# Ternary weights cast and summed in front of self attention, fp8 weights early, and a GpSimd wait at the attention seam

## The chip, the core and the metric

The kernel runs on one core of a Trainium2 chip. The metric is device time in microseconds for one execution, the median of several runs. TensorE (PE) does matrix products into PSUM, VectorE (DVE), ScalarE (ACT) and GpSimd (POOL) do elementwise work and reductions, SyncE (SP) issues most DMA transfers. Each engine runs its own list of instructions in order; semaphores hold an instruction until others are done.

## The reference

Eight residual stages run over x of 16 x 64 tokens and 256 features, each on the layer norm of x; `ctx` has the same shape.

```python
x = x + _L0_xattn_ref(16, 64, 256, L0_xattn_w, L0_xattn_u, _layernorm(x, axis=-1), ctx_2048)   # a decayed scan
x = x + _L0_ffn_ref(_layernorm(x, axis=-1), L0_ffn_W_gate, L0_ffn_W_qkv)                       # self attention, gated keys
x = x + _L1_xattn_ref(_layernorm(x, axis=-1), ctx_2048, ...)                                   # cross attention, int8 rounding
x = x + _L1_ffn_ref(_layernorm(x, axis=-1), L1_ffn_input2, L1_ffn_scale, L1_ffn_scale1)        # fp8 product
x = x + _L2_xattn_ref(_layernorm(x, axis=-1), ctx_2048, ctx_2048)                              # channel attention
x = x + _L2_ffn_ref(_layernorm(x, axis=-1), L2_ffn_w_gate_up, L2_ffn_w_proj)                   # ternary weights
x = x + _L3_xattn_ref(...)
x = x + _L3_ffn_ref(...)                                                                       # eight experts
```

The ternary weights of the sixth stage depend on no activation:

```python
w = w_fp32.astype(jnp.bfloat16)
w_g = w.reshape(-1, g)                                        # groups of 64
scale = jnp.clip(jnp.mean(jnp.abs(w_g), axis=-1, keepdims=True), 1e-08, None)
q = jnp.clip(jnp.round(w_g / scale), -1, 1)
w_hat = (q * scale).reshape(w.shape)
return w + jax.lax.stop_gradient(w_hat - w)
```

## The kernel before

The 1024 tokens are eight tiles of 128 (NT is 8). X holds the residual, XN the norms, both in SBUF throughout; `region` and `wide` are two large SBUF buffers out of which every stage cuts its own tiles. Each engine has one function per stage, called in order of the stages, so that the order of work on an engine is written out by hand, and semaphores tie the engines together. `x_done` counts finished residual tiles over all stages: the first stage ends at `x_done` 8. `ch.link` makes an instruction wait for the one before it on its own engine.

Self attention and cross attention are `pe_attention`, `act_attention`, `vec_attention` and `pool_attention` with s = 0 and s = 1. Each runs over the tiles with a fixed lag per step: `key_value` (TensorE), `select` (VectorE, from L703), key copy (`key_T`, L619, ScalarE), key blocks (`kbd`, L422, GpSimd), `scores` (L525, TensorE), `shift` (L737 and L740, VectorE), `probs` (L625), `probs_T`, `values` (L553), `normalise` (from L752). At the seam between the two, VectorE normalises and quantises the new tokens in halves: `quantise_norm` (L355 to L700), where TensorE waits for the second half in `quantised_T(1, 4)` ahead of the third scores. In the slot before that seam VectorE rounds the fp8 weights (`vec_f8_weights`, L838 to L396). GpSimd also splits the context into bf16 parts, a step per tile (`pool_context_part`, L991 to L999), adds biases to the values (L445) and fills a block with constants (`pool_blank_keys`).

Channel attention goes over 64 pairs of units in `pair_steps`: at pair w VectorE takes the maxima of its scores (L1171, two per pair); TensorE makes the scores of pair w (L1057) and, 13 pairs behind, the turned scores (L1081) and the values (L1097); ScalarE makes the exponentials (L1111). Three score banks are shared, so TensorE stops when VectorE has taken no maxima. Every eight pairs the maxima go through DMAs into the stack (`maxima_in`). Results go out to DRAM and come back per tile (`act_values_out`, `values_in`); VectorE inverts the sums (`invert`, L1187) and GpSimd multiplies and adds to X (`add_values`, L1153 and L1155).

The ternary weights are six chunks of 128 x 1024. Each is loaded (L1221 and L1225, ScalarE's queue, into two buffers in `wide`), cast to bf16 on ScalarE (L1231), summed by groups (L1241), scaled (L1243 to L1245), compared above and below (L1249, L1251) on VectorE, and put together by GpSimd (L1258 to L1261). Chunks 0 and 1 stand in front of VectorE's pair loop, 2 and 3 inside it, 4 and 5 after the second inversion. In `pe_ternary` TensorE turns the finished weights when all six are there; the stage's norm waits for all of X.

## Time and profile before

| what | us |
|---|---|
| median of 3 runs | 876.08 (875.85 to 881.13) |
| profiled execution | 883.72 |
| its span, first to last instruction | 881.9 |
| busy: PE / DVE / ACT / POOL | 653.6 / 519.7 / 285.3 / 248.6 |
| mean granted TensorE clock | 0.853 of full |

Times in the trace count from the start of the span of that one execution. The timeline lists instructions in order of time, several of one line in a row merged; a table of stretches gives busy time per engine between two times; groups by line add up instructions of one source line.

### The profile page before, as it was taken

What the parts mean: (1) busy time and instruction counts of PE and PEld (TensorE: products, weight loads), DVE (VectorE), ACT (ScalarE), POOL (GpSimd) and SP (SyncE); (2) the same over time, 40 slices, a digit from 0 to 9 for tenths busy, and PEclk for the clock granted to TensorE, in tenths of its full rate; (3) what the DMA queues carried; (4) which work ended last, traced back from release to release, by engine and by line L of the source; (5) the groups of instructions that cost most, each with busy time, mean ns of one, the idle gap of its engine ahead of it and who ended that gap; (6) DMA issues with size and microseconds to landing.
All of it is one profiled execution on the core that took longest, in us unless ns stands there. A gap on an engine that the chain in (4) does not pass through costs nothing.

```text
span 881.9 us, 10923 instructions
## 1 busy us (share of the span) xinstructions
PE 653.6 (74%) x3659; PEld 415.5 (47%) x3660; DVE 519.7 (59%) x1102; ACT 285.3 (32%) x522; POOL 248.6 (28%) x244
## 2 busy tenths in 40 slices
PE   2634888756883168989639996754599999999991
PEld 2323344533562115555334665524266666666661
DVE  6986687797969899998955444564321221212213
ACT  4811322313447106666624321331121121211210
POOL 3220432275901396130670005000212111121100
PEclk9665998677986559999958999975699999999996
DMA  7000003000206624561210002966000000000004
GB/s 239 0 0 1 0 1 72 1 1 0 61 1 156 157 70 107 136 169 47 66 48 1 1 1 99 430 267 253 24 19 30 30 24 24 25 30 30 18 12 156
DMA packets 34142, 61.85 MB, mean 70 GB/s; under 512 B 6232, under 2 KB 29784, under 8 KB 31768
## 3 DMA queue, kind: packets, MB, share of 16 engines
q1 hardware_dynamic: 22592, 45.78, 16.5%
q10 hardware_dynamic: 9296, 9.44, 3.5%
q0 software_dynamic: 2208, 6.03, 2.2%
q8 instruction: 26, 0.43, 0.2%
q14 instruction: 20, 0.16, 0.1%
HBM read 47.35 MB, written 13.50 MB: 69 GB/s over the span
## 4 chain that ended last, share of the span: by engine, by line
PE 48%; DVE 22%; issue 7%; POOL 5%; ACT 3%; DMA 1%; ACTq 0%; POOLq 0%; SPq 0%; DVEq 0%
PE bank L1746 16%; PE bank L1767 8%; PE bank L1386 5%; DVE region L1171 4%; PE bank L1405 3%; DVE XN L355 2%; PE bank L1757 2%; PE bank L553 2%; PE bank L525 2%; PE bank L1097 2%; PE bank L1057 1%; ACT region L1445 1%; PE bank L537 1%; POOL rstd L369 1%; PE bank L1081 1%
## 5 line engine op out<-in xcount | busy, mean ns | idle before, releaser
L1746 PE MATMUL bank<-region,wide 128*128 x368 | 144.0, 545 | 0.3 <-issue 0.3
L1650 DVE TENSOR_TENSOR wide<-wide,bank 128x448 f32<-128x448 f32 x46 | 28.6, 621 | 125.3 <-ACT wide L1693 125.3
L1746 PEld LDWEIGHTS bank<-region,wide 128*128 128x128 f32 x368 | 68.9, 192 | 61.6 <-issue 61.5
L1111 ACT ACTIVATE region<-bank 128x1024 f32<-128x1024 f32 x64 | 65.6, 1026 | 67.7 <-PE bank L1081 64.7
L1171 DVE TENSOR_REDUCE region<-bank 128x2 f32<-128x512 f32 x128 | 79.8, 678 | 7.1 <-PE bank L1057 6.9
L1767 PE MATMUL bank<-region,XN 128*128 x322 | 73.4, 379 | 1.2 <-DVE wide L1663 1.2
L1554 POOL DMA_INDIRECT choice_results<-wide,to_row x23 | 22.7, 987 | 181.6 <-DVE wide L1663 181.6
L1057 PE MATMUL bank<-region 128*128 128x256 bf16 x256 | 52.8, 305 | 20.4 <-DVE region L1171 15.9
L1767 PEld LDWEIGHTS bank<-region,XN 128*128 128x128 f32 x322 | 59.5, 190 | 9.3 <-issue 2.1
L1693 ACT ACTIVATE wide<-bank 128x448 f32<-128x448 f32 x46 | 25.0, 543 | 112.2 <-PE bank L1746 112.2
L369 POOL TENSOR_TENSOR rstd<-vareps,half_neg 128x4 f32<-128x4 f32 (+1 forms) x13 | 16.2, 1246 | 145.8 <-DVE vareps L365 96.3
L1881 PE MATMUL bank<-ident,XN 128*128 128x128 f32 x96 | 20.8, 398 | 42.0 <-DVE XN L355 26.5
L1657 DVE COPY XN<-bank 128x384 f32<-128x384 f32 x23 | 12.8, 557 | 63.2 <-PE bank L1757 63.2
L1386 PE MATMUL bank<-region 128*128 128x512 bf16 x192 | 44.3, 389 | 0.9 <-DVE region L404 0.9
L1097 PE MATMUL bank<-region 128*32 128x256 f32 x512 | 34.3, 383 | 12.9 <-ACT wide L1120 12.5
L1057 PEld LDWEIGHTS bank<-region 128*128 128x128 bf16 x256 | 19.8, 101 | 49.0 <-DVE region L1171 34.7
L553 PE MATMUL bank<-wide,region 128*64 128x34 f32 x512 | 33.4, 239 | 11.6 <-issue 8.8
L553 PEld LDWEIGHTS bank<-wide,region 128*64 128x64 f32 x512 | 32.0, 154 | 18.7 <-issue 15.8
L1881 PEld LDWEIGHTS bank<-ident,XN 128*128 128x128 f32 x96 | 17.9, 211 | 44.5 <-issue 26.9
L1081 PE MATMUL bank<-region 128*128 128x256 bf16 x256 | 38.2, 275 | 0.0
L1700 ACT ACTIVATE XN<-bank 128x512 f32<-128x512 f32 x23 | 13.7, 597 | 73.0 <-PE bank L1757 73.0
L422 POOL TENSOR_TENSOR region<-wide 128x1024 f32<-128x1024 f32 x16 | 30.5, 1925 | 22.0 <-DVE XN L700 11.4
(305 smaller groups left out, 1279.8 us busy)
## 6 DMA issues: line engine op xcount, KB each, us to landing
region<-in_L_ffn_experts_dram SPq DMA_DIRECT2D x8, 2688.0 KB, 19.2
region<-ctx_parts SPq DMA_DIRECT2D x24, 192.0 KB
region<-norm_parts SPq DMA_DIRECT2D x24, 192.0 KB
channel_values<-wide ACTq DMA_DIRECT2D x8, 512.0 KB, 4.4
ctx_parts<-region SPq DMA_DIRECT2D x40, 64.0 KB, 2.1
wide<-in_L_ffn_w_gate_up_dram ACTq DMA_DIRECT2D x4, 512.0 KB, 7.1
wide<-channel_values SPq DMA_DIRECT2D x16, 128.0 KB, 2.6
norm_parts<-region SPq DMA_DIRECT2D x24, 64.0 KB, 4.6
```

Of the source, the lines that this page charges most:

```text
L422: last = e.tensor_tensor(KBD[i % 2][c], src.unsqueeze(1).broadcast_to([P, HC, P]), headmask.unsqueeze(2).broadcast_to([P, HC, P]), ALU.mult)
L553: last = e.matmul(ps(4 + i % 2, w * j, w * j + w)[T * b:T * b + T, :], PT[:, P * j + T * b:P * j + T * b + T], VBD[i % 2][:, b, 0 if s == ...
L1057: last = e.matmul(score_bank("scores", n)[:, D * mc:D * mc + D], QS[i % RING][:, n % TU, P * mc:P * mc + P], KS[i % RING][:, n % TU, :], s ...
L1081: last = e.matmul(ps(2 + 2 * (w % 2) + u, D * nc_, D * nc_ + D), KS[i % RING][:, n, P * nc_:P * nc_ + P], QS[i % RING][:, n, :], start=Tru ...
L1097: last = e.matmul(ps(6, 0, D)[32 * g:32 * g + 32, :], flat[:, 2 * DH * n:2 * DH * n + 32], PT5[(2 * q + g // 2) % 4][:, 512 * (g % 2) + D ...
L1111: e.activation(PT5[w % 4], bank[1 + w % 2][:, :], ACT.Exp, scale=QSCALE).then_inc(s_chan["probs_ready"], 1)
L1171: e.tensor_reduce(nmax[i % 2][:, at_:at_ + KC], score_bank("scores", n).rearrange("p (c n) -> p c n", c=KC), AX.X, ALU.max, negate=True).t ...
L1386: last = e.matmul(bank[hf][:, 512 * gu:512 * gu + 512], x6[j][:, c, P * i:P * i + P], guT[:, c, lo:lo + 512], start=(j == 0 and c == 0), s ...
L1650: e.tensor_tensor(HB8[par][:, cols], silu8[:, cols], bank[hf][:, 512:512 + I8 // 2], ALU.mult)\
L1746: last = e.matmul(bank[hf][:, 512 * gu:512 * gu + hw], xbT[par][:, P * c:P * c + P], region[:, bass.ds(off + (2 * gu + c) * I8 + hw * hf, ...
L1767: last = e.matmul(ps(7, 0, D), HT8[par][:, P * k:P * k + P], region[:, bass.ds(off + 4 * I8 + D * k, D)], start=(k == 0), stop=(k == I8 // ...
L1881: last = e.transpose(ps(first + c, P * j, P * j + P), src[:, D * i + P * c:D * i + P * c + P], ident[:, :])
```

## The change

The six chunks get six buffers of their own, in the place of the later key stacks 2 and 3 and the fill block in `region`. SP loads them all behind the fp8 weights, when the first residual is done, and issues the context parts after that. ScalarE casts the chunks ahead of the loop of self attention, around its first gate sum and its query copies. VectorE rounds the fp8 weights and makes the sums of chunks 0 and 1 before the first `select`, the sums of the other four and the scales of all after it. In channel attention only the two comparisons of each chunk are left on VectorE, at pairs 3 and 4, 12 and 13, and so on every nine; nothing of the ternary weights is in front of the loop or behind it. GpSimd puts all six chunks together before it adds any values, and VectorE adds the last tile's values itself. At the seam GpSimd waits for all quantised norms before it goes on with the context parts and key block 2.

```diff
-        traw = [wide[:, TCH * j:TCH * j + TCH] for j in range(2)]
+        traw = [carve(TCH, at=STACK * 2 + TCH * c) for c in range(TW // TCH)]
...
                     if i == 1:
                         pool_norm(e, 2, 4, NT)
+                        e.wait_ge(s_att["norm_quantised"], NT)
                     pool_context_part(e, ch, 1, i - 1)
...
             if s == 0:
-                gate_sum(0)
-                leave(QT, 0, s_att["q_in_psum"], s_att["q_ready"])
+                for c in range(TW // TCH):
+                    if c == 2:
+                        gate_sum(0)
+                    if c == 4:
+                        leave_half(QT, 0, 0, s_att["q_in_psum"], s_att["q_ready"])
+                    act_ternary_cast(e, c)
+                leave_half(QT, 1, KC, s_att["q_in_psum"], s_att["q_ready"])
...
+                if s == 0 and t == 0:
+                    vec_f8_weights(e, ch)
+                    for c in range(2):
+                        vec_ternary_sums(e, ch, c)
                 if s == 0 and t < NT:
                     select(t)
+                if s == 0 and t == 0:
+                    for c in range(2, TW // TCH):
+                        vec_ternary_sums(e, ch, c)
...
                 if s == 0 and t == NT + 1:
                     quantise_norm(0, 4)
-                if s == 0 and t == NT + 2:
-                    vec_f8_weights(e, ch)
                 if s == 0 and t == NT + 3:
                     e.wait_ge(x_done, 2 * NT)
                     norm_variance(e, ch, 2, 4, NT, first=NT - 1)
...
             act_blanks(e, KS[2:4], True)
-            for c in range(2):
-                act_ternary_load(e, c)
             e.wait_ge(s_att["projected"], NT)
             act_blanks(e, QS[0:2], False)
             turned_f8(0)
             act_blanks(e, QS[2:4], True)
-            for c in range(2):
-                act_ternary_cast(e, c)
-                act_ternary_load(e, c + 2)
...
         def values_in(e, i):
             e.wait_ge(s_chan[f"values_stored{i % 2}"], 16 * (i // 2 + 1))
-            if i == 2:
-                e.wait_ge(s_tern["weights_cast"], 5)
             if i >= SETS:
                 e.wait_ge(x_done, 4 * NT + i - SETS + 1)
             v = o_dram[i].rearrange("q (g r) d -> (q g) r d", g=4)
...
             if i == RING:
+                e.wait_ge(s_tern["weights_cast"], TW // TCH)
                 ch.link(e.memset(fill5[0:32, :].bitcast(U32), 0))
             elif i == RING + 1:
...
-            def weights(w):
-                if w in CASTS:
-                    c = CASTS[w]
-                    act_ternary_cast(e, c)
-                    if c + 2 < TW // TCH:
-                        act_ternary_load(e, c + 2)
-
-            CASTS = {8: 2, 16: 3, 24: 4, 32: 5}
-            pair_steps([(weights, 0), (probs, BEHIND), (values, BEHIND + 2), (values_out, BEHIND + 2)])
+            pair_steps([(probs, BEHIND), (values, BEHIND + 2), (values_out, BEHIND + 2)])
...
         def pool_channel_tiles(e, ch):
-            WEIGHTS = {0: (0, 1, 2, 3), 2: (4,), 4: (5,)}
             for i in range(2, NT):
                 e.wait_ge(s_chan["norm_split"], i)
                 split_q(e, ch, i, qrest[1])
-            for i in range(NT):
-                for c in WEIGHTS.get(i, ()):
-                    pool_ternary_weights(e, ch, c)
+            for c in range(TW // TCH):
+                pool_ternary_weights(e, ch, c)
+            for i in range(NT - 1):
                 add_values(e, ch, i)
 
         def add_values(e, ch, i):
             e.wait_ge(s_chan["sums_inverted"], i + 1)
             ch.link(e.tensor_tensor(NUM5[i % SETS], NUM5[i % SETS], DEN5[i % SETS], ALU.mult))
+            if i == NT - 1:
+                e.wait_ge(x_done, 4 * NT + i)
             xi = X[:, D * i:D * i + D]
             e.tensor_tensor(xi, xi, NUM5[i % SETS], ALU.add).then_inc(x_done, 1)
 
         def vec_channel(e, ch):
-            WEIGHTS = {17: 2, 35: 3}
-            for c in range(2):
-                for step in range(4):
-                    vec_ternary_step(e, ch, c, step)
+            SIGNS = {9 * c + 3: c for c in range(TW // TCH)}
...
             def weights(w):
-                for first, c in WEIGHTS.items():
-                    if 0 <= w - first < 4:
-                        vec_ternary_step(e, ch, c, w - first)
+                for step in range(2):
+                    if w - step in SIGNS:
+                        vec_ternary_signs(e, ch, SIGNS[w - step], step)
 
             pair_steps([(maxima, 0), (maxima_parts, 1), (weights, 0)])
             for i in range(NT):
                 invert(i)
-                if i == 1:
-                    for c in (4, 5):
-                        for step in range(4):
-                            vec_ternary_step(e, ch, c, step)
+            add_values(e, ch, NT - 1)
...
-        def act_ternary_load(e, c):
-
-            if c >= 2:
-                e.wait_ge(s_tern["weights_cast"], c - 1)
+        def sp_ternary_load(e, c):
...
+                e.dma_start(traw[c].rearrange("p (r d) -> p r d", d=D),
                             L2_ffn_w_gate_up[P * rows * c:P * rows * (c + 1), :].rearrange("(r p) d -> p r d", p=P))\
-                    .then_inc(s_tern[f"weights_loaded{c % 2}"], 16)
...
         def act_ternary_cast(e, c):
-            e.wait_ge(s_tern[f"weights_loaded{c % 2}"], 16 * (c // 2 + 1))
-            if c == 0:
-                e.wait_ge(x_done, 3 * NT)
-            e.activation(tern[:, ternary_slices(c)[0]], traw[c % 2], ACT.Copy).then_inc(s_tern["weights_cast"], 1)
-
-        def vec_ternary_step(e, ch, c, step):
+            e.wait_ge(s_tern[f"weights_loaded{c // 2}"], 32)
+            e.activation(tern[:, ternary_slices(c)[0]], traw[c], ACT.Copy).then_inc(s_tern["weights_cast"], 1)
+
+        def vec_ternary_sums(e, ch, c):
+            cols, g = ternary_slices(c)
+            e.wait_ge(s_tern["weights_cast"], c + 1)
+            last = e.tensor_reduce(tscale[:, g], by_group(tern[:, cols]), AX.X, ALU.add, apply_absolute_value=True)
+            if c == TW // TCH - 1:
+                ch.link(last)
+                ch.link(e.tensor_scalar(tscb, tscale, 1.0 / GROUP, 1e-8, ALU.mult, ALU.max))
+                e.tensor_scalar(thigh, tscb, 0.5 + 2.0 ** -9, None, ALU.mult)
+                ch.link(e.tensor_scalar(tlow, tscb, -(0.5 + 2.0 ** -9), None, ALU.mult))
+
+        def vec_ternary_signs(e, ch, c, step):
 
             cols, g = ternary_slices(c)
             w = tern[:, cols]
             if step == 0:
-                e.wait_ge(s_tern["weights_cast"], c + 1)
-                if c == 0:
-                    e.wait_ge(x_done, 4 * NT)
-                ch.link(e.tensor_reduce(tscale[:, g], by_group(w), AX.X, ALU.add, apply_absolute_value=True))
-            elif step == 1:
-                ch.link(e.tensor_scalar(tscb[:, g], tscale[:, g], 1.0 / GROUP, 1e-8, ALU.mult, ALU.max))
-                e.tensor_scalar(thigh[:, g], tscb[:, g], 0.5 + 2.0 ** -9, None, ALU.mult)
-                ch.link(e.tensor_scalar(tlow[:, g], tscb[:, g], -(0.5 + 2.0 ** -9), None, ALU.mult))
-            elif step == 2:
                 if c >= 2:
                     e.wait_ge(s_tern["weights_ternary"], c - 1)
                 e.tensor_tensor(by_group(tpos[c % 2]), by_group(w), spread(thigh[:, g]), ALU.is_gt)
...
-            for i in range(NT // 2):
-                sp_context_parts(e, i)
             e.wait_ge(x_done, NT)
...
-            for i in range(NT // 2, NT):
+            for c in range(TW // TCH):
+                sp_ternary_load(e, c)
+            for i in range(NT):
                 sp_context_parts(e, i)
             sp_first_keys(e)
```

## Rows read from the trace of the kernel before

**Rows 1.** Timeline, front of self attention: start us, us, engine, line, operation, out<-in, count
```profile
74.92 1.28 DVE L2037 TENSOR_TENSOR X<-X,bank 128x512 f32<-128x512 f32 x2
...
79.52 1.38 DVE L355 TENSOR_SCALAR XN<-X,meanvar,rstd 128x256 f32<-128x256 f32 x4 [1.19 <-POOL rstd L369]
...
87.05 0.17 DVE L711 COPY region<-bank 128x16 f32<-128x16 f32 x1 [6.15 <-PE bank L491]
...
94.41 0.27 ACT L619 ACTIVATE region<-bank 128x128 f32<-128x128 f32 x1
```
**Rows 2.** Stretches: us, busy PE PEld DVE ACT POOL (instructions), PEclk, DMA share, GB/s
```profile
2.50:20.00 17.50, 3.70 (x17) 3.43 (x17) 13.18 (x41) 8.93 (x14) 5.20 (x13) 0.96 0.89 300
...
176.70:185.70 9.00, 7.93 (x40) 5.01 (x40) 8.72 (x11) 1.37 (x2) 6.46 (x5) 0.69 0.01 2
...
304.50:314.30 9.80, 0.00 (x0) 0.00 (x0) 9.59 (x14) 0.00 (x0) 9.08 (x11) 0.50 0.60 134
...
333.00:418.00 85.00, 75.40 (x797) 46.60 (x798) 77.15 (x142) 57.59 (x77) 23.44 (x12) 1.00 0.46 116
```
**Rows 3.** Timeline, the seam between self and cross attention
```profile
167.34 1.37 DVE L355 TENSOR_SCALAR XN<-X,meanvar,rstd 128x256 f32<-128x256 f32 x4
...
172.31 1.14 DVE L700 TENSOR_SCALAR XN<-XN,region 128x256 f32<-128x256 f32 x4
...
185.80 3.65 PE L525 MATMUL bank<-region 128*64 128x512 f32 x16 [0.98 <-ACT region L1966]
...
188.04 1.22 DVE L737 TENSOR_REDUCE region<-bank 128x16 f32<-128x1024 f32 x1
...
189.28 1.04 POOL L991 CAST region<-region 128x1024 bf16<-128x1024 f32 x1
...
190.40 3.80 POOL L422 TENSOR_TENSOR region<-wide 128x1024 f32<-128x1024 f32 x2
190.43 6.84 DVE L355 TENSOR_SCALAR XN<-X,meanvar,rstd 128x256 f32<-128x256 f32 x4
...
203.95 1.14 DVE L700 TENSOR_SCALAR XN<-XN,region 128x256 f32<-128x256 f32 x4
...
207.11 3.15 PE L525 MATMUL bank<-region 128*64 128x512 f32 x8
...
241.78 2.88 PE L525 MATMUL bank<-region 128*64 128x512 f32 x8
```
**Rows 4.** Groups by line, VectorE, 333 to 418: count, busy us, mean ns, idle before, releaser
```profile
L1171 DVE TENSOR_REDUCE region<-bank 128x2 f32<-128x512 f32 x100 | 62.9, 679 | 7.0 <-PE bank L1057 6.7
```
**Rows 5.** Timeline, the end of channel attention
```profile
447.78 1.75 DVE L1187 RECIPROCAL wide<-wide 128x256 f32<-128x256 f32 x1 [1.03 <-DMA wide<-channel_values]
...
449.45 1.34 DVE L344 BATCH_NORM_STATS2 stats<-X 128x6 f32<-128x256 f32 x4
...
455.56 0.72 POOL L1155 TENSOR_TENSOR X<-X,wide 128x256 f32<-128x256 f32 x1
```
**Rows 6.** Ternary steps: a group (304.5 to 314.3), then single lines (ns min/median/max)
```profile
L1241 DVE TENSOR_REDUCE region<-region 128x16 f32<-128x1024 bf16 x2 | 2.4, 1206 | 0.0
...
L1231 ACT ACTIVATE region<-wide x6: 1048/1056/1058, 281.6 to 364.0; 128x1024 bf16<-128x1024 f32 x6
...
L1249 DVE TENSOR_TENSOR region<-region x6: 1212/1225/1226, 306.7 to 432.7; 128x1024 bf16<-128x1024 bf16 x6
...
L1251 DVE TENSOR_TENSOR region<-region x6: 1211/1456/3151, 307.8 to 433.8; 128x1024 bf16<-128x1024 bf16 x6
```
**Rows 7.** Groups by line, GpSimd, 185 to 240
```profile
L422 POOL TENSOR_TENSOR region<-wide 128x1024 f32<-128x1024 f32 x12 | 22.5, 1899 | 10.5 <-PE bank L525 10.2
L445 POOL TENSOR_TENSOR wide<-wide,region 128x256 f32<-128x256 f32 x6 | 4.4, 742 | 0.0
L997 POOL TENSOR_TENSOR region<-region 128x1024 f32<-128x1024 f32 x1 | 2.1, 2132 | 0.1
```
**Rows 8.** DMA issues on the page: line, count, KB each, median us to landing
```profile
wide<-in_L_ffn_w_gate_up_dram ACTq DMA_DIRECT2D x4, 512.0 KB, 7.1
```

4 lines of the change are left out of this document (2 added, 2 removed).

## Prediction

> **What bounds the kernel now.** No engine bounds the whole: each stage has its own limit. So I read the timeline of the three places that the diff touches, and the table of stretches to see which engine has room in them.
>
> - *In front of self attention.* The first residual is complete when the two adds that start at 74.92 end, at 76.2. VectorE then makes norms until 80.9 and does nothing until 87.05, when TensorE has made the first keys and values and `select(0)` begins. ScalarE's next serial step is the key copy at 94.41 [rows 1].
> - *The attention seam.* VectorE never rests here: the fp8 weight rounding fills a stretch of 9.00 us (8.72 busy) [rows 2], then come the first shift of cross attention at 188.04 and the quantisation of the second half of the tokens. That of the first half began at 167.34 and ended at 172.31 + 1.14 = 173.45: 6.1 us. The second began at 190.43 and ended at 203.95 + 1.14 = 205.1: 14.7 us. Beside the second GpSimd ran its context parts and key blocks (L991 at 189.28, L422 at 190.40 and on). TensorE waits for that half and makes its third scores at 207.11 [rows 3].
> - *Channel attention.* Between 304.5 and 314.3 VectorE is busy for 9.59 us and TensorE not at all [rows 2]: these are the eight ternary steps of chunks 0 and 1, and the first maximum stands behind them. From 333 to 418 VectorE is busy for 77.15 of 85.00 us and TensorE for 75.40 [rows 2]; VectorE's maxima wait 7.0 us in all, nearly always for TensorE [rows 4]. Both are close to the limit.
> - *The end of that stage.* VectorE inverts the last sums at 447.78, but GpSimd is still in the last ternary chunk, so its last add starts at 455.56; the statistics for the next norm can't end before it [rows 5].
>
> Later stages are not touched: they move as a block.
>
> **Part by part, in us; minus is gained.**
>
> *Front: +1.0.* VectorE gets the fp8 rounding and two group sums ahead of `select(0)`. The rounding took 9.0 at the seam beside GpSimd; shrunk as the quantisation did, 6.1 to 14.7, it is 3.7. GpSimd has nothing to do here until `select(0)` is through, so I take 4.5, above that ratio: from 80.9 to 85.4. Two sums at 1.206 [rows 6] end at 87.85, and `select(0)` is 0.8 late. The casts on ScalarE cost 1.056 each [rows 6]: two before the gate sum, where ScalarE waits for VectorE anyway, two after it and two between the halves of the query copy; half of these four finds gaps, and I put the key copy at 95.4 to 95.5. Behind it stand GpSimd's key block, the first scores and VectorE's first shift, a serial chain, so +1.0 is passed on to the end. The other four sums (4.8) and the three scale instructions lie between `select(0)` and `select(1)`, where VectorE waits for the next keys; without that gap they would cost 5.5 more.
> All this holds if the weights are there. The six loads and the fp8 load are 3.4 MB. At the start of the program 300 GB/s came in over 17.5 us [rows 2]: 11.4 us from 77.8, when SP has issued the small ones, so the third pair lands near 90, ahead of casts 4 and 5 at about 92. Ends: +0.4 (full cover) and +5.5 (rounding still 9.0). On SP the context parts stand behind the loads; they wait for GpSimd's split, which begins only inside self attention: nothing.
>
> *fp8 out of the seam: -0.4.* The last normalise of self attention, its variance and GpSimd's rstd come 5 us earlier, but then the first shift waits for scores: TensorE's run of 16 starts at 185.80 and takes 3.65, so the first eight are done at 187.65 [rows 3]. The shift goes from 188.04 to 187.7. What hides the rest is TensorE's query projection.
>
> *GpSimd's wait: -5.2.* Behind it stand a context cast (1.04), key block 2 (two L422 of 1.899), the value biases and all later key blocks [rows 3, 7]. VectorE, alone, needs 6.1 instead of 14.7: from 190.1 to 196.3, and its own gain would be 8.8. But GpSimd starts its cast only then: 196.4 + 1.1 + 4.0 = 201.5 for key block 2, and the third scores wait for that. 207.11 becomes 201.5: 5.6 with the fp8 part. From there I followed GpSimd: a tile is a value bias of 0.742, at the longest a context part of 2.13, and a key block of 3.8, 6.7 in all; five more end at 235.0 at the latest. The last scores, made at 241.78, need the last of them at 241.78 - 5.6 = 236.2 [rows 3, 7]. GpSimd keeps over 1 us in hand, so the 5.6 go through to the end of cross attention. Ends of the two parts together: -3.0 (GpSimd sets the pace) and -8.8.
> By the Trainium skill (GPSIMD Engine Reference, section "Key points") GpSimd shares its SBUF interfaces with VectorE, and collides with VectorE's instructions in a two-port mode or with two SBUF inputs. Here the trace agrees: four L355, with one SBUF input, went from 1.37 to 6.84 us [rows 3]. Without such a collision the wait would gain nothing, and the sum below would be -6.3.
>
> *Front of the channel loop: -9.8.* The stretch 304.5 to 314.3 [rows 2] goes. The first scores are there: TensorE does nothing in that stretch, since its score banks are full and wait for the maxima. With the ternary loads out of the DMA queues the first stacks land no later.
>
> *Signs in the loop: +6.4.* Each chunk keeps its two comparisons. L1249 takes 1.225; L1251 took 1.211 to 3.151, median 1.456 [rows 6]. Chunks 0 and 1 now stand at pairs 3, 4, 12 and 13, where the loop fills and VectorE alone sets its pace, and GpSimd works beside both: I take 1.7 for L1251, above its median, so 2 x (1.23 + 1.72) = 5.9. Chunks 2 to 5 add 4 x 2.42 = 9.7 to the stretch after 333, from which the whole of chunks 2 and 3 goes at about 4.1 each (the stretch 304.5 to 314.3 has two for 9.6, beside GpSimd): +1.5 of work for VectorE, against 7.0 of waiting for TensorE [rows 4]. I take +0.5, nearer to full cover, since the new pieces are shorter and further apart. ScalarE loses four casts there; taken at nothing, as it is not the limit. Ends: +3 and +13 (a rival).
>
> *Tail: -3.5.* GpSimd's chunks 4 and 5 are done long before. The last inversion, to 447.78 + 1.75 = 449.5, waits for a DMA and moves only with the rest. VectorE then does the two instructions of the last add itself, about 1.0, and eight statistics at 1.34 for four, 2.7: 453.2. Before, the last add ended at 455.56 + 0.72 and one statistic followed: 456.7 [rows 5]. The wait of that add on the seven others holds nothing, as they end before the last inversion. Ends: -2 and -5.
>
> The wait for the casts in GpSimd's blanking is met 100 us earlier. The turning of the ternary weights on TensorE comes earlier, into a gap, and frees nothing that the norm doesn't hold.
>
> **Sum:** 1.0 - 0.4 - 5.2 - 9.8 + 6.4 - 3.5 = -11.5. The profiled execution, 883.72, would be 872.2; it was 7.6 above the median of the runs shown, 876.08, so there I forecast **864.6**.
>
> **Rivals.**
> 1. *Signs and GpSimd collide in the loop.* If all four comparisons of chunks 0 and 1 take the longest L1251 seen, 3.15, they cost 12.6 instead of 5.9: sum -4.8, 871.3. For it: L1251's spread [rows 6]. Against: L1249 stood at 1.21 to 1.23 in all six [rows 6]. By the skill's section named above both comparisons, with two SBUF inputs, should suffer; that is this case.
> 2. *The seam gives half.* GpSimd, held back, becomes the bound of cross attention: -3.0 there, sum -8.9, 867.2. For it: only 1 us in hand by the longest parts. Against: two of five parts are casts of 1.04.
> 3. *Slower than before: the loads are late.* Casts 2 to 5 stand in front of ScalarE's key copy and their sums in front of `select(1)`, so every microsecond past 92 goes to the end. In the old kernel a 512 KB load took 7.1 in the median [rows 8], beside other traffic. Six of them one behind the other, 42.6, would land at 120.4: front 1.0 + 28.4 = 29.4, sum +16.9, 893.0. It turns the sign once the last pair lands after 104, a rate under 130 GB/s. Against: 300 GB/s at the start, with as many loads queued [rows 2].
>
> **Chances and range.** Forecast 0.70, rival 1 0.12, rival 2 0.12, rival 3 0.04, 1 and 2 together 0.02. About 1%, 8.8 us, is what a measurement of this kernel can tell from no change: under 867.3 is faster. Nine tenths of the forecast and half of rival 2 lie there: 0.69. Slower is rival 3, 0.04. The rest, 0.27, is within. The best ends, 0.4 - 8.8 - 9.8 + 3 - 5, give -20, 856; with rivals 1 and 2 the top is 872. Range 856 to 872.
>
> **What would show it.** Six casts between 83 and 95 with no long wait; the key copy near 95.5; the four L355 of the second half in 1.4; third scores 5 us earlier; the first maximum right behind the norms; sign pieces of 1.2 to 1.7; the last add on VectorE within 1.5 of the last inversion. Wrong would be: ScalarE waiting for DMA at the casts; TensorE's scores waiting for L422 in every tile; L1171 waiting for TensorE more than 7 in the loop, which would mean that the loop has another bound.

## The result

The changed kernel takes 875.0 us in the median of 20 runs (869.4 to 879.5). The kernel before took 877.6 in 20 runs beside them (875.5 to 887.1). The ratio is 0.994 with an interval of 0.992 to 0.996, some 5 us. The medians are only 2.6 us apart, the means 4.4 (879.3 and 874.9): eight of the 20 executions of before take over 880, none of after. 11.5 us were forecast, and 875.0 lies outside the range of 856 to 872.

The profiled execution of after took 875.02 us, with a span of 872.9. Against the profiled execution of before, 883.72, that is 8.7 less. But that execution of before was a long one. A second profiled execution of the same kernel, taken in the first experiment, has a span of 874.6 us. The table has the start of the same instruction in all three (the end, for the last maximum), from the timelines.

| us | before, 881.9 | before again, 874.6 | after, 872.9 | after minus before again |
|---|---|---|---|---|
| first selection | 87.05 | 86.53 | 88.05 | +1.5 |
| last shift of self attention | 162.93 | 159.64 | 161.71 | +2.1 |
| third scores | 207.11 | 203.84 | 201.20 | -2.6 |
| first reciprocal of cross attention | 216.61 | 213.24 | 212.41 | -0.8 |
| last reciprocal of cross attention | 260.27 | 254.41 | 254.68 | +0.3 |
| first maximum | 314.30 | 308.44 | 298.95 | -9.5 |
| end of the last maximum | 418.16 | 412.96 | 413.61 | +0.7 |
| norm behind channel attention | 459.51 | 454.34 | 450.18 | -4.2 |
| first product of two expert halves | 635.00 | 627.62 | 625.80 | -1.8 |
| end of the span | 881.9 | 874.6 | 872.9 | -1.7 |

Now the profile after. The timeline in front of self attention (start us, us, engine, line, operation, out<-in, count); it answers [rows 1]. The first line is the residual add, L717 are the selections, L1223 the sums, L1226 the scale, L1218 the casts, L620 the key copy:

```profile
75.16 1.28 DVE L2025 TENSOR_TENSOR X<-X,bank 128x512 f32<-128x512 f32 x2
...
85.79 2.34 DVE L1223 TENSOR_REDUCE region<-region 128x16 f32<-128x1024 bf16 x2
88.05 0.17 DVE L717 COPY region<-bank 128x16 f32<-128x16 f32 x1
...
91.47 4.59 DVE L1223 TENSOR_REDUCE region<-region 128x16 f32<-128x1024 bf16 x4
96.09 1.26 DVE L1226 TENSOR_SCALAR region<-region 128x96 bf16<-128x96 f32 x1
...
97.75 0.17 DVE L717 COPY region<-bank 128x16 f32<-128x16 f32 x1
...
91.61 1.99 ACT L1218 ACTIVATE region<-region 128x1024 bf16<-128x1024 f32 x2
...
95.04 0.27 ACT L620 ACTIVATE region<-bank 128x128 f32<-128x128 f32 x1
```

Fp8 rounding and two sums hold the first selection back to 88.05; four sums and the scale hold the second back to 97.75. Casts and key copy stand where they were forecast.

The seam, against [rows 3] (L743 the shift, L355 and L706 first and last step of the second quantisation, L422 key block 2, L526 the third scores, L1876 the query product):

```profile
187.69 1.22 DVE L743 TENSOR_REDUCE region<-bank 128x16 f32<-128x1024 f32 x1 [5.13 <-PE bank L526]
...
190.09 1.37 DVE L355 TENSOR_SCALAR XN<-X,meanvar,rstd 128x256 f32<-128x256 f32 x4
...
195.07 1.14 DVE L706 TENSOR_SCALAR XN<-XN,region 128x256 f32<-128x256 f32 x4
...
196.28 1.04 POOL L995 CAST region<-region 128x1024 bf16<-128x1024 f32 x1 [12.53 <-DVE XN L706]
197.40 3.75 POOL L422 TENSOR_TENSOR region<-wide 128x1024 f32<-128x1024 f32 x2
...
201.20 3.68 PE L526 MATMUL bank<-region 128*64 128x512 f32 x8 [2.90 <-POOL region L422]
204.81 4.87 PE L1876 MATMUL bank<-region 128*128 128x512 f32 x8
```

The four L355 take 1.37 us in place of 6.84, and the second quantisation ends at 196.2. GpSimd starts then, and the scores wait 2.90 us for its key block, as forecast (201.5). But these scores take 3.68 us and the query product behind them 4.87.

Stretches of after (us, busy PE PEld DVE ACT POOL, granted clock, DMA share, GB/s), against [rows 2]. The first is the front with its loads, the second the seam without fp8, the last two belong to the channel loop:

```profile
79.00:91.50 12.50, 10.31 (x26) 5.98 (x27) 10.89 (x27) 6.25 (x10) 0.72 (x1) 0.73 0.77 253
176.70:185.70 9.00, 8.03 (x33) 4.32 (x32) 3.42 (x10) 1.37 (x2) 6.03 (x5) 0.63 0.00 0
316.00:330.00 14.00, 11.16 (x62) 5.83 (x61) 12.03 (x18) 4.37 (x5) 13.61 (x7) 0.62 0.06 15
...
391.00:395.00 4.00, 3.74 (x26) 1.83 (x27) 2.69 (x5) 0.47 (x2) 3.84 (x3) 0.57 0.14 45
```

The loads come at 253 GB/s without holding anybody up long. Two stretches of the loop stand out: from 316 to 330 and from 391 to 395 TensorE was granted 0.62 and 0.57 of its clock on average, most of the time the lower of its two levels, 1.2 GHz, while it had work. Before, the clock of the loop from 333 on was full [rows 2]. In the first part of the loop it was low before as well: in before again for 19.7 us from the first maximum on (308.44 to 328.17), in after for 20.9 us (298.95 to 319.85) and once more from 323.26 to 330.09.

VectorE's maxima from 333 to 418 (group by line: count, busy us, mean ns, idle before, releaser) wait 8.3 us for TensorE, where it was 7.0 [rows 4]; the forecast had named more than 7 as the sign that the loop has another bound:

```profile
L1166 DVE TENSOR_REDUCE region<-bank 128x2 f32<-128x512 f32 x91 | 57.3, 680 | 8.3 <-PE bank L1062 8.2
```

The end of channel attention, against [rows 5]: last inversion, the two instructions of the last add, statistics, all on VectorE:

```profile
442.11 1.75 DVE L1182 RECIPROCAL wide<-wide 128x256 f32<-128x256 f32 x1 [8.20 <-DMA wide<-channel_values]
443.90 0.42 DVE L1149 TENSOR_TENSOR wide<-wide 128x256 f32<-128x256 f32 x1
444.36 0.42 DVE L1153 TENSOR_TENSOR X<-X,wide 128x256 f32<-128x256 f32 x1
444.70 2.70 DVE L344 BATCH_NORM_STATS2 stats<-X 128x6 f32<-128x256 f32 x8
```

And the prices (ns min/median/max), against [rows 6]: casts, sums, and the two comparisons:

```profile
L1218 ACT ACTIVATE region<-region x6: 1040/1045/1057, 84.5 to 92.6; 128x1024 bf16<-128x1024 f32 x6
L1223 DVE TENSOR_REDUCE region<-region x6: 1207/1209/1214, 85.8 to 94.8; 128x16 f32<-128x1024 bf16 x6
L1237 DVE TENSOR_TENSOR region<-region x6: 1203/1216/2144, 303.7 to 387.1; 128x1024 bf16<-128x1024 bf16 x6
L1239 DVE TENSOR_TENSOR region<-region x6: 1202/1216/1939, 306.1 to 389.4; 128x1024 bf16<-128x1024 bf16 x6
```

### The profile page after: what moved, and what is told of

Its sections match the earlier page's. It is cut to its first block, busy times and chain, and to the rows that moved or that the text cites. A ratio compares the mean times of both kernels' runs of the same rounds, so it can differ in the third digit from the quotient of the medians.

```text
span 872.9 us, 10888 instructions
## 1 busy us (share of the span) xinstructions
PE 652.2 (75%) x3645; PEld 413.5 (47%) x3660; DVE 502.8 (58%) x1089; ACT 285.8 (33%) x522; POOL 245.1 (28%) x242
## 4 chain that ended last, share of the span: by engine, by line
PE 49%; DVE 20%; issue 9%; POOL 3%; ACT 3%; DMA 2%; SPq 0%; POOLq 0%; ACTq 0%; DVEq 0%
PE bank L1734 16%; PE bank L1755 8%; PE bank L1374 5%; DVE region L1166 4%; PE bank L1393 3%; PE bank L1102 3%; PE bank L1745 2%; PE bank L554 2%; PE bank L526 1%; ACT region L1433 1%; PE bank L1086 1%; DVE XN L355 1%; PE bank L1062 1%; POOL region L422 1%; POOL rstd L369 1%
## 5 line engine op out<-in xcount | busy, mean ns | idle before, releaser
L1166 DVE TENSOR_REDUCE region<-bank 128x2 f32<-128x512 f32 x128 | 80.1, 678 | 10.2 <-PE bank L1062 10.1
L1062 PE MATMUL bank<-region 128*128 128x256 bf16 x256 | 54.3, 311 | 17.7 <-DVE region L1166 16.2
L1869 PE MATMUL bank<-ident,XN 128*128 128x128 f32 x96 | 20.9, 399 | 39.6 <-DVE XN L355 33.4
L1086 PE MATMUL bank<-region 128*128 128x256 bf16 x256 | 39.6, 283 | 0.0
L526 PE MATMUL bank<-region 128*64 128x512 f32 x128 | 35.3, 657 | 5.7 <-POOL region L422 3.8
```

The source lines that it names most:

```text
L526: last = e.matmul(sbank(i)[rows, 512 * c:512 * c + 512], QT[:, c, P * i + T * b:P * i + T * b + T], KBD[i % 2][0 if s == 0 else c][:, :, T ...
L1062: last = e.matmul(score_bank("scores", n)[:, D * mc:D * mc + D], QS[i % RING][:, n % TU, P * mc:P * mc + P], KS[i % RING][:, n % TU, :], s ...
L1086: last = e.matmul(ps(2 + 2 * (w % 2) + u, D * nc_, D * nc_ + D), KS[i % RING][:, n, P * nc_:P * nc_ + P], QS[i % RING][:, n, :], start=Tru ...
L1166: e.tensor_reduce(nmax[i % 2][:, at_:at_ + KC], score_bank("scores", n).rearrange("p (c n) -> p c n", c=KC), AX.X, ALU.max, negate=True).t ...
L1869: last = e.transpose(ps(first + c, P * j, P * j + P), src[:, D * i + P * c:D * i + P * c + P], ident[:, :])
```

## The experiments

Theory: what was forecast for the sections of the code is right in kind, but (a) TensorE's granted clock changes from one execution to the next, and the profiled execution of before was a long one; (b) what is gained at the seam is lost to that clock behind the wait; (c) the signs cost far more in the loop than 6.4 us, because of where they stand. The rivals are named in each expectation. The ratios are to the kernel before, run beside each (its medians there are 878.4 to 878.9). Differences to after are to its 875.0 above.

| run | median us | ratio | interval |
|---|---|---|---|
| before_again | 879.7 | 1.002 | 0.999 to 1.006 |
| wait_only | 876.1 | 0.995 | 0.992 to 0.998 |
| no_wait | 878.2 | 0.997 | 0.994 to 1.000 |
| warm_seam | 870.2 | 0.990 | 0.985 to 0.994 |
| short_signs | 858.8 | 0.976 | 0.972 to 0.980 |
| spread_signs | 857.5 | 0.976 | 0.971 to 0.980 |
| fill_signs | 868.4 | 0.988 | 0.985 to 0.991 |
| row_signs | 857.6 | 0.976 | 0.973 to 0.979 |
| late_signs | 866.8 | 0.988 | 0.984 to 0.992 |
| seam_sums | 872.7 | 0.991 | 0.987 to 0.995 |
| all_waits | 857.0 | 0.976 | 0.971 to 0.980 |
| spread_warm | 854.3 | 0.972 | 0.970 to 0.975 |

### The kernel before, once more

No edit.

> The kernel before, unchanged, to see where its executions of 876 and of 884 us differ. If the profiled execution of before was long because TensorE's granted clock was low from 155.0 to 161.8 us, where it was full in the kernel after, a short execution has the full clock there and its last shift of self attention comes at about 160 instead of 162.9, and the seam and the first maximum lie the same distance behind it. If the seam itself is what varies, the four L355 of the second half take less than 6.84 us in a short execution and the third scores come less than 44 us behind the last shift of self attention.

Measured: its twelve executions take 875.9 to 887.4 us, and time and mean granted clock go together: the five from 875.9 to 876.6 have a clock of 0.871 to 0.873, the three over 886 have 0.854. The profiled one is short (876.39). Where the two executions of before part is in the table above: 3.3 us up to the last shift of self attention, 2.6 more in cross attention, 2.7 in front of the experts; elsewhere 1.3 go the other way, which makes 7.3. The first and the last are TensorE's clock, as the next lines show; for the second the long execution has a stretch at the low clock from 250.5 to 257.4 that the short one hasn't there. The end of self attention in the long and then in the short execution:

```profile
150.00:163.00 13.00, 11.62 (x68) 5.97 (x66) 8.31 (x24) 3.82 (x13) 3.19 (x3) 0.74 0.01 2
```

```profile
147.00:160.00 13.00, 11.61 (x87) 6.16 (x85) 10.29 (x28) 5.05 (x15) 3.01 (x4) 1.00 0.10 27
```

0.74 against 1.00. And the gate product in front of the experts (PE, 32 matmuls), long, then short:

```profile
600.57 6.99 PE L1712 MATMUL bank<-wide 128*128 128x8 f32 x32 [0.69 <-ACT wide L1964]
```

```profile
595.55 4.96 PE L1712 MATMUL bank<-wide 128*128 128x8 f32 x32 [0.69 <-ACT wide L1964]
```

6.99 against 4.96 us, the same 32 instructions. The granted clock in the short execution is full for part of this product; in the long one it is at the lower level throughout. After's profiled execution is of the longer sort here:

```profile
591.38 7.00 PE L1700 MATMUL bank<-wide 128*128 128x8 f32 x32 [0.69 <-ACT wide L1952]
```

So the difference of the two profiled executions, 8.7 us, is not the effect of the change; 7.3 us lie between two executions of one kernel. What makes an execution of before go the one way or the other isn't known; the trace shows it only by its clock.

### GpSimd's wait alone, and after without it

```diff
+                        e.wait_ge(s_att["norm_quantised"], NT)      # wait_only: before with this line
-                        e.wait_ge(s_att["norm_quantised"], NT)      # no_wait: after without it
```

> The kernel before with GpSimd's wait alone. If the wait is worth what the prediction says, it gains 5.2 us less what the fp8 rounding in front of the seam now delays: 3 to 5 us, ratio 0.994 to 0.997. If the seam's gain is lost again further on (GpSimd as the bound of cross attention), 0 to 1.5 us.

> The kernel after without GpSimd's wait: 5 us slower than after by the prediction (about 880), the third scores 5 us later relative to the last shift of self attention. If the wait gives nothing in a usual execution, the same time as after, 875.

Measured: the wait gains 0.5% on before (4.3 us, 1.5 to 7.1 by the interval), and taking it out of after loses 0.3% (0.997 against 0.994, about 3 us, though the two intervals overlap). That is the order of the forecast, a little under it. In no_wait the third scores come 43.0 us behind the last shift of self attention (164.53 to 207.51) and the last reciprocal of cross attention 96.1, where after has 39.5 and 93.0: 3.5 later at the scores, where 5 were expected. In the traces it shrinks on its way: between the last shift of self attention and the third scores wait_only needs 39.5 us (159.83 to 199.34) and before again 44.2 (159.64 to 203.84), 4.7 less; to the first reciprocal of cross attention 2.9 less are left, to the last one 1.8. The third scores and the query product of before again:

```profile
203.84 2.64 PE L525 MATMUL bank<-region 128*64 128x512 f32 x8
206.82 3.70 PE L1888 MATMUL bank<-region 128*128 128x512 f32 x8 [0.34 <-ACT region L1964]
```

In after, and in wait_only alike, they take 3.68 and 4.87 to 4.88. The clock came up at 205.3 us in before again and at 205.4 in wait_only, though TensorE began its scores 4.5 us earlier in the second. Ahead of the rise it had turned the second half at 201.97 and gone straight on in before again; in wait_only it had turned it at 194.50 and then stood idle for 2.9 us in front of the scores. The work that starts earlier ran longer at 1.2 GHz.

### TensorE kept busy at the seam

```diff
                     e.wait_ge(s_att["out_normalised"], NT)
+                    for _ in range(5):
+                        e.matmul(ps(4), wqT[:, 0, 0:P], XT[:, 0, 0:512], start=True, stop=True)
                     quantised_T(1, 4)
...
             def scores(i):
+                if s == 1 and i == 2:
+                    e.wait_ge(s_att["scores_shifted"], NT + 1)
+                    for _ in range(2):
+                        e.matmul(ps(0), wqT[:, 0, 0:P], XT[:, 0, 0:512], start=True, stop=True)
                 e.wait_ge(s_att["key_blocks"], NT * s + i + 1)
```

> The kernel after with seven products of no use on TensorE while it waits at the seam: five in front of the second half's turning, two in front of the third scores; they write banks that are overwritten. If the gain of GpSimd's wait is lost to TensorE's low clock behind the idle time (third scores 3.68 instead of 2.64, query product 4.88 instead of 3.70), the granted clock is full at 201 us, the first values of cross attention come 2 us earlier relative to the last shift of self attention than in after (50.7 there), and the time is about 873. If GpSimd's key blocks are what binds, the third scores start at the same 201 us and nothing behind them moves: 875.

Measured: 870.2, 4 to 5 us less than after, more than expected. (The intervals of the two ratios overlap a little; spread_warm, below, repeats the gain: all its runs are shorter than any of spread_signs.) Stretches of after, then of this run, the wait and what comes behind it (columns as above):

```profile
189.00:201.00 12.00, 3.39 (x18) 2.42 (x16) 9.96 (x20) 4.57 (x9) 4.64 (x3) 0.69 0.00 1
201.00:212.00 11.00, 9.93 (x45) 4.19 (x45) 2.45 (x2) 3.06 (x8) 10.70 (x9) 0.72 0.00 0
```

```profile
189.00:201.00 12.00, 8.44 (x32) 4.43 (x34) 9.30 (x20) 4.73 (x9) 5.30 (x4) 1.00 0.00 1
201.00:212.00 11.00, 9.81 (x64) 4.80 (x60) 5.37 (x11) 5.32 (x12) 10.70 (x8) 1.00 0.00 0
```

The timeline of its third scores and query product:

```profile
200.54 1.94 PE L530 MATMUL bank<-region 128*64 128x512 f32 x8 [1.90 <-POOL region L422]
202.41 3.70 PE L1882 MATMUL bank<-region 128*128 128x512 f32 x8
```

The granted clock is full, the scores take 1.94 and the query product 3.70. The scores start no earlier: 39.5 us behind the last shift of self attention, in both. So GpSimd's key block sets their start, as the prediction had it, and the clock takes the gain back behind them. The first reciprocal of cross attention comes 47.7 us behind that shift in place of 50.7, and the last one 89.4 in place of 93.0. That the low clock is what took the seam's gain back is shown.

### The signs cut short

```diff
-                e.tensor_tensor(by_group(tpos[c % 2]), by_group(w), spread(thigh[:, g]), ALU.is_gt)
+                e.tensor_tensor(by_group(tpos[c % 2])[:, 0:1], by_group(w)[:, 0:1], spread(thigh[:, g])[:, 0:1], ALU.is_gt)
```

and the same for `is_lt`.

> The kernel after with each of the twelve comparisons cut to 64 of its 1024 columns, so the ternary weights are not the reference's; all else is done. By the prediction the signs cost 6.4 us in the loop, so about 869. By the comparison of the two traces they cost 10.8 (6.2 in the fill, 1.6 for chunks 2 to 5, 3.0 at two places where TensorE runs behind and at the low clock), so about 864 to 865. If another limit stands behind VectorE, less than 4 us are gained: over 871.

Measured: 858.8, 16 us less than after, more than either figure. The loop, from the start of the first maximum to the end of the last, is 102.3 us (298.90 to 401.23) where after has 114.7, so 12.3 of it; the rest is the clock behind the loop (the ternary stage begins 1.7 us sooner after its norm, the experts 2.7 sooner after theirs). And even these comparisons of 64 columns aren't free where GpSimd works: 0.20 to 0.23 us in most places, but in the fill of the loop (two lines of VectorE, then the two GpSimd products beside them):

```profile
316.21 1.61 DVE L1237 TENSOR_TENSOR region<-region 128x64 bf16<-128x64 bf16 x1
...
318.94 1.08 DVE L1239 TENSOR_TENSOR region<-region 128x64 bf16<-128x64 bf16 x1
...
315.84 1.90 POOL L1247 TENSOR_TENSOR region<-region 128x1024 bf16<-128x1024 bf16 x1
317.82 2.12 POOL L1248 TENSOR_TENSOR region<-region 128x1024 bf16<-128x1024 bf16 x1
```

The first ends at 317.82, the second at 320.02: each 0.08 us behind a GpSimd instruction (317.74 and 319.94).

### The signs where VectorE waits

```diff
-            SIGNS = {9 * c + 3: c for c in range(TW // TCH)}
+            SIGNS = {8 * c + 21 + 2 * step: (c, step) for c in range(TW // TCH) for step in range(2)}
```

`weights(w)` looks up the chunk and the comparison of pair w there, here and in the runs below.

> The kernel after with the comparisons at other pairs: none in the fill of the loop, one at every second pair from 21 to 63, in front of the places where VectorE waits 0.2 to 0.8 us for TensorE in the run with short signs; the two of a chunk no longer stand one behind the other. If a comparison costs what is left of it when VectorE's own wait there is taken off, and the rest of the 12.4 us is TensorE's low clock behind two comparisons in a row, this gains 5 to 8 us on after: 867 to 870, and no low clock between 330 and 410 us. If VectorE and TensorE are so locked together that a comparison costs its whole 1.2 us wherever it stands, twelve of them are 13 and the time is that of after, 874 to 876.

Measured: 857.5, 17 us less than after and beyond both expectations. The loop is 102.0 us (296.63 to 398.60), no longer than with signs cut short. VectorE's maxima over the whole loop in after:

```profile
L1166 DVE TENSOR_REDUCE region<-bank 128x2 f32<-128x512 f32 x128 | 80.1, 678 | 10.2 <-PE bank L1062 10.1
```

and here:

```profile
L1166 DVE TENSOR_REDUCE region<-bank 128x2 f32<-128x512 f32 x128 | 79.2, 679 | 1.6 <-PE bank L1062 1.5
```

The stretch of the fill here that answers the one of after from 316 to 330:

```profile
314.00:328.00 14.00, 13.29 (x140) 8.49 (x138) 13.32 (x25) 9.64 (x12) 0.00 (x0) 0.99 0.15 35
```

Twelve full comparisons are 14.6 us of work, and the idle time ahead of the maxima falls from 10.2 to 1.6 us: the work went where VectorE had waited for TensorE. In after the same work stood elsewhere, and the waits stayed. In the fill the clock is 0.99 where it was 0.62, and it isn't low again before 427.0, as was expected.

### Which of the places was it?

```diff
+            # fill_signs
+            SIGNS = {9 * c + 3 + step if c < 2 else 8 * c + 5 + 2 * step: (c, step) for c in range(TW // TCH) for step in range(2)}
...
+            # row_signs
+            SIGNS = {8 * c + 21 + step: (c, step) for c in range(TW // TCH) for step in range(2)}
```

> The run with spread signs, but the comparisons of chunks 0 and 1 back at pairs 3, 4, 12 and 13 as in after; those of chunks 2 to 5 stay apart, at pairs 21 to 47. If signs in the fill cost what the traces say (2.2 for chunk 0, 1.4 for chunk 1, and 2.3 more where TensorE runs behind them at the low clock), the loop is 5 to 6 us longer than the 101.3 of the run with spread signs and the time is 862 to 864. If the fill was not the matter, 857 to 859.

> The run with spread signs, but the second comparison of each chunk one pair earlier, right behind the first pair's (21 and 22, 29 and 30, to 61 and 62). If it is the second one in a row that costs (it stands where VectorE has no wait, and TensorE runs dry behind it), each of six costs 1.0 to 1.2 us more and some end in a low clock for 1 to 2 us: loop 108 to 112, time 864 to 869. If only the fill and not the order was the matter, loop 101 to 103 and 857 to 859.

Measured: with chunks 0 and 1 back in the fill the loop is 110.0 us (296.31 to 406.26), 8.0 longer than in spread_signs, where 5 to 6 were expected; the time is 868.4, since the ternary stage behind the loop starts 2.4 us later after its norm as well; with the two comparisons at neighbouring pairs the loop is 103.0 (298.58 to 401.59) and the time 857.6. The fill of fill_signs:

```profile
313.00:328.00 15.00, 12.34 (x67) 6.18 (x71) 12.96 (x20) 4.89 (x6) 14.61 (x7) 0.62 0.06 15
```

So it is the fill, and it is not that the two follow each other: by the times of the maxima against those of short_signs, the second one in row_signs costs 1.0 to 1.1 us when it runs, but 0.7 to 0.9 of that comes back at VectorE's next wait. In after chunks 2 to 5 stand at pairs counted in nines, while VectorE's waits come at the same two or three of every eight pairs; some stand behind a wait with no other near and get nothing back. By subtraction these four chunks cost 4.7 us in after (114.7 less 110.0). By the starts of the maxima in the two traces chunks 2 to 4 cost 1.1 of it together, and chunk 5, at pairs 48 and 49, costs 3.6 alone: both its comparisons are paid nearly whole (2.3), and 1.4 more go at pairs 51 to 53, where TensorE's clock is low (391.52 to 394.94). That the low clock costs these 1.4 is read off the trace; no run tried it by itself. The expectation that neighbours are dear was wrong.

### Signs behind the loop

```diff
             for i in range(NT):
                 invert(i)
+                add_values(e, ch, i)
+                if i < 2:
+                    for step in range(2):
+                        vec_ternary_signs(e, ch, 4 + i, step)
```

with chunks 0 to 3 as in spread_signs and no add on GpSimd.

> The same with chunks 4 and 5 compared behind the loop, where VectorE waits 14 us for the last stored values, and all last adds on VectorE so that GpSimd is free for those two chunks. If signs cost nothing in that wait and the tail stays bound by the last values, 2 to 3 us less than the run with spread signs: 864 to 867. If GpSimd's last chunk now ends behind VectorE's last add (the rival that made the tail of before), the tail takes back 3 us or more: 868 to 871.

Measured: 866.8, 9 us more than with all signs in the loop. It lies in the first range that was expected by luck alone: that range was counted from 867 to 870 for spread_signs, which took 857.5. The tail lost most of it: the last inversion comes 35.5 us behind the last maximum's start (29.1 in spread_signs), and not for GpSimd's last chunk, which ends at 424.4, but on VectorE, which is busy without a break from 400 to 434. Its instructions before and while GpSimd runs a ternary chunk (L1149 the add, L1235 a comparison), then one of the GpSimd products beside them:

```profile
402.26 0.42 DVE L1149 TENSOR_TENSOR X<-X,wide 128x256 f32<-128x256 f32 x1
402.60 1.22 DVE L1235 TENSOR_TENSOR region<-region 128x1024 bf16<-128x1024 bf16 x1
...
407.47 2.00 DVE L1149 TENSOR_TENSOR X<-X,wide 128x256 f32<-128x256 f32 x1
409.40 3.15 DVE L1235 TENSOR_TENSOR region<-region 128x1024 bf16<-128x1024 bf16 x1
...
409.27 2.19 POOL L1246 TENSOR_TENSOR region<-region 128x1024 bf16<-128x1024 bf16 x1
```

An add of 0.42 takes 2.00, a comparison of 1.22 takes 3.15. The inversions (one input, 1.73 to 1.75) don't stretch.

### VectorE's work out of the front

```diff
-                if s == 0 and t == 0:
-                    vec_f8_weights(e, ch)
-                    for c in range(2):
-                        vec_ternary_sums(e, ch, c)
...
+                if s == 1 and t == 0:
+                    vec_f8_weights(e, ch)
+                if s == 1 and t == 3:
+                    for c in range(4):
+                        vec_ternary_sums(e, ch, c)
                 for f, lag in ((shift, 1 + L), (normalise, 3 + L), (probs_T, 2 + L)):
+                    if s == 1 and t == 3 and f is normalise:
+                        for c in range(4, TW // TCH):
+                            vec_ternary_sums(e, ch, c)
```

The four sums behind `select(0)` go too. The fp8 rounding now stands behind self attention's last normalise, four sums in front of the third shift of cross attention, two sums and the thresholds behind it.

> The kernel after with the fp8 rounding and the six group sums taken out of VectorE's work in front of self attention and put where VectorE waits at the seam (5.1, 5.7 and 5.0 us idle in after); casts and loads stay in front. By the comparison of the traces the front cost 2.1 us against a usual execution of before, 1.0 by the prediction. If that is VectorE's work ahead of its first two selections, the last shift of self attention comes 1.5 us earlier than in after and the time is 873 to 874. If it is the casts on ScalarE and the loads, that shift stays at 161 to 162; if the sums stretch beside GpSimd, the seam takes the gain back: 875 to 877.

Measured: 872.7, 2 us less than after, with intervals that overlap. The last shift of self attention comes at 159.79, 1.9 earlier than in after and as in before again, as was expected if the front's cost was VectorE's work. But that isn't shown: spread_signs, fill_signs and late_signs keep all of this work in front and reach the same shift at 159.25, 158.95 and 158.65. The first threshold step and the second selection of spread_signs, which stand at 96.09 and 97.75 in after:

```profile
95.75 0.69 DVE L1225 TENSOR_SCALAR region<-region 128x96 bf16<-128x96 f32 x1
...
96.84 0.17 DVE L717 COPY region<-bank 128x16 f32<-128x16 f32 x1
```

From the first residual's add to the first shift before again needs 24.3 us, this run 24.4, those three 25.0, and the other six executions with the front of after 25.5 to 26.0. So 0.7 is VectorE's work. The rest goes with TensorE's clock: it is low until 85.2 to 85.7 in the three, until 86.4 to 87.7 in the six.

The fp8 rounding is hidden in the seam: the third scores come 39.6 us behind the last shift of self attention, in after 39.5. But the seam takes part back. VectorE around the first reciprocal of cross attention, the last line:

```profile
205.14 2.34 DVE L1224 TENSOR_REDUCE region<-region 128x16 f32<-128x1024 bf16 x2
...
207.95 1.94 DVE L1228 TENSOR_SCALAR region<-region 128x96 f32<-128x96 bf16 x1
209.82 1.93 DVE L1229 TENSOR_SCALAR region<-region 128x96 f32<-128x96 bf16 x1
211.78 0.26 DVE L758 RECIPROCAL region<-bank 128x16 f32<-128x16 f32 x1
```

The two last threshold instructions, 0.21 and 0.20 long in after, run beside GpSimd's key block (L422, 207.94 to 211.69) and take 1.94 and 1.93; the reciprocal comes 52.0 us behind the last shift of self attention, in place of 50.7, and the last reciprocal 95.3 in place of 93.0. At the first maximum this run is 0.4 us behind after (299.34); it gets ahead only in the channel loop, which takes 112.3 us in place of 114.7 though nothing in it was changed. So no gain from emptying the front is shown.

### Together

spread_warm is spread_signs with the lines of warm_seam. all_waits is spread_warm with these (four sums stay behind `select(0)`, the thresholds are a function of their own):

```diff
-                    vec_f8_weights(e, ch)
-                    for c in range(2):
-                        vec_ternary_sums(e, ch, c)
...
+                if s == 1 and t == 0:
+                    vec_ternary_limits(e, ch)
+                    vec_f8_weights(e, ch)
                 for f, lag in ((shift, 1 + L), (normalise, 3 + L), (probs_T, 2 + L)):
+                    if s == 0 and t == NT + 3 and f is normalise:
+                        for c in range(4, TW // TCH):
+                            vec_ternary_sums(e, ch, c)
```

> Spread signs and the seven products of no use at the seam together. If both gains are what they look like (12.7 in the loop, 3.6 between the last shift of self attention and the last reciprocal of cross attention), they add: 852 to 855. If part of the loop's gain was the granted clock of stages that neither edit touches, they do not add fully: 856 to 858.

> The same, and VectorE's work in front of self attention moved into its waits: fp8 rounding and thresholds behind the last normalise of self attention (GpSimd idles there), four sums behind the first selection, two in front of the last reciprocal of self attention. If the front's 1.9 us was that work, the last shift of self attention comes 1.5 us earlier than with spread signs and products of no use and the time is 850 to 853. If the seam takes it back, 853 to 856.

Measured: spread_warm 854.3 (853.1 to 854.9 in six runs, ratio 0.972): the two gains add within 2 us, and it is the shortest of all. The first and the last reciprocal of cross attention come 47.7 and 89.4 us behind the last shift of self attention, as in warm_seam, and the loop takes 101.9 us (102.2 in all_waits), as in spread_signs. all_waits, with the front emptied as well, 857.0, no better: its first selection comes at 86.49 and its first shift at 99.10, as early as in before again, but in the profiled execution TensorE's clock was low three times in self attention, and the last shift came at 164.29, 3.8 later than in spread_warm. Its six runs fall into two groups, 853.5 to 854.8 (clock 0.881 to 0.888) and 859.2 to 862.4 (0.869 to 0.877). That step was expected to gain and did not.

## Why the prediction was wrong, step by step

Measured is after against before again, an execution of after at its median and one of the shorter ones of before (876.39).

- **The sum and its base.** The sum was made from the long execution and taken off 876.08. That is sound only if the change saves the same in a short one. After's usual execution pays in front of the experts (the gate product of 7.00 us) what before's short one doesn't and its long one does: +2.5 us that no term had, from the norm behind channel attention (-4.2) to the end (-1.7).
- **Front, +1.0: measured +2.1.** 0.4 was there at the first residual's add, ahead of the change. From that add to the first shift after needs 26.0 us, before again 24.3: 1.7. VectorE's work is sized right: spread_signs, fill_signs and late_signs, with the same front, need 25.0, 0.7 more than before again (0.8 forecast), and their second selection comes 9.1 us behind the first, as in before again, so the four sums and the thresholds are covered. The other 1.0 goes with TensorE's clock, low until 87.74 in after: the key copy and GpSimd's key block come 1.0 later behind the add than in spread_signs, and the first threshold step, beside that block, takes 1.26 in place of 0.69. The term left out that clock.
- **Fp8 and wait, -5.6: measured -1.8.** Every row that the step named came out: L355 in 1.37, GpSimd at 196.28, the third scores at 201.20, 4.7 us nearer to the last shift of self attention than before. The step that failed is that "the 5.6 go through to the end of cross attention". It followed GpSimd and left out TensorE's clock: 2.2 us go in the scores and the query product; the rest goes by the last reciprocal, where after has two stretches at 1.2 GHz (224 to 228, 248 to 252) and before again had one (243 to 246). With TensorE kept busy (warm_seam) the last reciprocal is 5.4 us nearer to the last shift of self attention than in before again (89.4 against 94.8), which is what the step had forecast; the two later stretches weren't tried by themselves. (In all seven profiled executions with the wait at the seam, without the products of no use and with VectorE's work in front or as before, that distance is 92.9 to 93.2.) Rival 2 was nearer in size (-3.0), but it named another cause; GpSimd was not the bound.
- **Front of the channel loop, -9.8: measured -9.8** (+0.3 to -9.5).
- **Signs in the loop, +6.4: measured +10.2** (-9.5 to +0.7). It splits by the experiments: +8.0 for chunks 0 and 1 in the fill (110.0 less 102.0), where 5.9 was forecast (by the starts of the maxima in these two runs 2.5 at chunk 0, 3.7 at chunk 1 and 2.4 at pairs 14 to 20 behind them, of which 0.6 comes back); +4.7 for chunks 2 to 5, less 2.5 for the two chunks that left (before again has 104.5), all over the 102.0 of spread_signs; so +2.2 where 0.5 was. The failed step is the cover: "1.5 of work for VectorE, against 7.0 of waiting". A sum of waits hides work only where the work stands in front of a wait; in after the waits remained and grew to 8.3. The two old chunks, by the forecast's own count 8.2 us of work, had cost only 2.5 over that loop. The prices were nearly right: both comparisons of chunk 0 at 1.25 and 1.41, of chunk 1 at 2.14 and 1.94, beside GpSimd, which is part of rival 1. What no price held are the 2.4 us behind them, where TensorE's clock was low (up to 317.49 and from 320.90 to 327.73 in fill_signs, up to 314.38 in spread_signs); that the clock is their cause no run tried by itself. spread_signs has the loop that the forecast was thinking of, and a better one: 2.5 us shorter than before's.
- **Tail, -3.5: measured -4.8** (+0.7 to -4.2). The last add is on VectorE 0.04 us behind the last inversion, as forecast. But that inversion came 1.0 nearer to the end of the last maximum too, which no term had. It waits for the loads of the last tile, which SP issues 25.5 us behind that end in after and 26.4 in before again, though the store that they read is issued at 22.5 in both. In before again the loads of the tile in front stand 0.2 us ahead of this store (435.31): their buffer was set free by GpSimd's third add, which stood behind a ternary chunk until 435.2. In after they stand 8.0 us ahead of it. That the two transfers delay each other isn't shown.

The sum: 2.1 - 1.8 - 9.8 + 10.2 - 4.8 + 2.5 = -1.6, against -1.7 in the spans. The range was also narrower than the rivals that it names: 1 and 2 together give -2.2, 873.9, above its top of 872.

Of the three signs that the forecast named against itself two were quiet: ScalarE waited 0.7 us for the first weights, and TensorE's scores waited long for GpSimd once, at the third. The third, more than 7 us of waiting in the loop, spoke, but it was a weak sign (before again has 7.7 from 325 to 413), and not one of another bound: the waits vanish in spread_signs.

## What to carry to other kernels

Work that is to vanish in an engine's waits must be placed in front of a wait that the trace shows, again and again, or a pair ahead of one, and the proof is that the wait shrinks; the same twelve comparisons made the loop 12.7 us longer in one order than in another. Where a change makes TensorE's work start earlier after a wait, forecast it at the clock that the stretch had, not at full clock, and try a few products of no use in the wait. Take a second execution of the kernel before, and sort both by granted clock, before summing terms. A step of 1 us can't be read from one execution of each kernel: the last shift of self attention came anywhere from 158.7 to 164.5 with the same code in front of it.

## What the runs showed of the hardware

- One program, executed 66 times, took 875.6 to 887.9 us, and the mean granted clock of TensorE went along: 0.871 to 0.873 in the six shortest, 0.853 to 0.854 in the six longest. Single stages change by 2 to 3 us with it.
- Seven useless products of 512 columns on TensorE made the kernel 4 to 5 us shorter (870.2 against 875.0), and 3 us with the signs spread (854.3 against 857.5).
- VectorE waited for GpSimd by whole instructions: a comparison of 64 columns (0.2 us alone) took 1.61 and 1.08 us and ended with GpSimd's instruction; an add of 0.42 took 2.00; a threshold step of 0.21 took 1.94; an inversion of 1.75 was never longer. The Trainium skill says as much (SBUF — State Buffer, section "SBUF: two separate sides"): the shared ports are locked for a whole instruction and the other engine stands still. The trace agrees, with those numbers, for the two-input operations and for the threshold steps. That VectorE and GpSimd share their SBUF interfaces, as the Trainium skill has it in GPSIMD Engine Reference, section "Key points", on which the prediction drew, fits the four L355: 6.84 us beside GpSimd, 1.37 with GpSimd held back.
